# Linear attention: lengths and angles in groups among the projections, lookup and statistics among the pairs, an own output buffer; setup loads in another order

## The chip, the cores and the metric

The kernel runs on 1 core of one Trainium2 chip. The metric is the device time of one execution, in microseconds (us), lower is better.

## The reference, cut to what matters

2048 tokens of 512 features go through six residual layers. `_layernorm` and `ffn`, `attn` are as below; the change touches the second layer and what surrounds it.

```python
x = x + 0.5 * L0_ffn(layernorm(x))      # a lookup: each token picks one of 64 tiles, 8 features get a spline value
x = x + L0_attn(layernorm(x))           # linear attention
x = x + 0.5 * L0_ffn(layernorm(x))      # the same lookup
x = x + 0.5 * L1_ffn(layernorm(x))      # gate, up and down product with Hadamard-turned weights
x = x + L1_attn(layernorm(x))
x = x + 0.5 * L1_ffn(layernorm(x))

def L0_attn(x):                          # 4 sequences of 512, 16 heads of 32, 8 heads for k and v
    q, k, v = (x @ W.T + b for W, b in ...)
    q, k = rotate(q), rotate(k)          # q * cos + rotate_half(q) * sin
    def kernel(x):                       # length, projection, sine and cosine
        x = x / max(sqrt(sum(x * x)), 1e-6)
        p = x @ rand_matrix.T
        return concat(sin(p), cos(p)) / sqrt(32)
    kv = einsum('bhsf,bhsd->bsfd', kernel(k), v)      # for each token, over its heads
    out = einsum('bhsf,bsfd->bhsd', kernel(q), kv)
    return out @ Wo.T + bo
```

## The kernel before, in words

The program is written by hand for five queues: TensorE (pe), VectorE (V, dve), ScalarE (act), GpSimd (pool) and SyncE (sp), which issues all copies. Each queue runs in the order in which its code is written; named semaphores tie them. All tiles are cut by hand from one SBUF tensor, `arena`, and PSUM is one tensor `ps` of 8 banks of 512 floats, so rows of the trace read arena and ps, and it is the line that tells the operation.

The tokens are worked in 4 chunks of 512 (`NCH`). The stages, in order:

- **Setup** (`setup_*`): loads x and all weights, turns the weights by transposes (`first` for three groups of the attention weights, `turned` for the others, lines 776 and 917), mixes them with Hadamard matrices, and routes the first lookup. GpSimd mixes W_down, after ScalarE scaled it in `scale_down` (line 792). One set of statistics over all 16 token tiles (`setup_stats_vector`, `setup_scale_vector`, `setup_norm_vector`) feeds it. SyncE's order of loads is in `setup_sync`.
- **Linear attention** (`b_tensor`, `b_scalar`, `b_vector`, `b_pool`, `b_sync`), chunk by chunk. Per chunk: the products of the values (4 token tiles, line 1189, VectorE adds the bias at 1411); 6 blocks z of 128 rows for keys and queries, with 12 products each (1189), bias on ScalarE (1318), cosine product on GpSimd (1368), rotation product (1229), sine product and sum on VectorE (1421, 1422), square on GpSimd (1372) and sum of squares per head (1234), all six blocks into one bank. Then the lengths for all 24 heads at once: maximum (1430), root (1333) and `rsqrt_vector` (a reciprocal at 350 and three steps that refine it). Then for each block the angle product (1258), a product that spreads 1/length over the head's rows (1261), a copy (1330), multiply, round and subtract on VectorE (1439, 1445, 1447), the sine (1340), a cast (1343) and the low half (1451). `b_sync` sends values to DRAM and back, and issues 36 copies (1391) that put the features of the tokens side by side. Then 16 pairs of groups of tokens: scores (1277), mask on VectorE (1460), product with the values (1287); every four pairs ScalarE and VectorE split the result into a high and a low half (1354, 1485). It goes into `ht_hi` and `ht_lo`, the buffers that hold the chunk's normalized input. Last the output product (1189) and the residual (1475, 1478).
- Among this stands work for other chunks. `last` is the chunk before: its second statistics and routing (`token_stats_*`, `route_*`) stand among the projections. `next` is the chunk after: its first lookup (`apply_*`, `spline_vector`, lines 1035 to 1086) stands between the last low half and the pairs, and adding it to x (`add_vector`, 1002 to 1023) and the statistics (`norm_stats_vector`, `norm_scale_vector`) stand behind the pairs. Its transposes (`norm_tensor`, 1167, casts 1158 and 1127) stand behind the output product, in banks 0 and 1 in turn.
- Chunks 1 and 2 are one hardware loop (`Fori`), chunks 0 and 3 are written out. In the loop the semaphore values are registers (`gate`).
- Then the last routing, and four passes of the large products and the second attention, unchanged.

## Time and profile before

| | us |
|---|---|
| median of 3 runs (lowest, highest) | 2493.17 (2491.18, 2495.68) |
| the profiled execution, its own time | 2493.57 |
| its span in the trace | 2491.8 |
| busy in the span: TensorE, VectorE, ScalarE, GpSimd | 2077.4, 1250.5, 743.3, 200.6 |
| start of the first chunk's values, of the fourth's, of the stage behind the attention | 300.12, 745.57, 949.14 |

The profile is of one execution. An engine is busy while an instruction runs; register, semaphore and DMA-issuing instructions are not counted. The granted clock is that of TensorE as a share of 2.4 GHz. A row of the timeline merges neighbours of one line.

### The profile page before, as it was taken

Reading aid. Unit: us, or ns where it says so; the run is one execution under the profiler, and the core shown is the slowest. Engines: PE = TensorE matmul, PEld = TensorE weight load, DVE = VectorE, ACT = ScalarE, POOL = GpSimd, SP = SyncE. Lnnn points to the kernel's source line nnn. Section 1 sums busy time; section 2 is a strip of 40 time slices with the busy share of each in tenths; the row PEclk is TensorE's granted clock in tenths of the full one; section 3 lists DMA queues with packets and bytes.
Section 4 is the critical chain, followed back from the end, with each engine's and each line's share of the span. In section 5 each row is a group of like instructions: output and inputs, shape, how many; then the busy total and the mean of one; then the engine's idle time right before and its main releaser. Section 6 shows DMA issues by size and latency. Waiting matters only on the chain. (4 is left out here: it accounts for less than half of the span.)

```text
span 2491.8 us, 30544 instructions
## 1 busy us (share of the span) xinstructions
PE 2077.4 (83%) x12014; PEld 981.1 (39%) x12014; DVE 1250.5 (50%) x2301; ACT 743.3 (30%) x1146; POOL 200.6 (8%) x148
## 2 busy tenths in 40 slices
PE   4777477756658548999999999999999999999998
PEld 3444224223223224444444444444444444444443
DVE  4444456364464444645456625662567355633332
ACT  4443131223212312222323522352235223521211
POOL 3340010101002000000000101000100010000000
PEclk8777577767678668999999999999999999999999
DMA  6211420111001311222210211121112111222322
GB/s 255 68 51 17 167 37 22 7 39 17 23 16 17 106 69 62 97 96 85 77 43 29 77 56 35 34 77 51 42 35 77 51 43 34 71 74 100 104 99 87
DMA packets 90978, 158.70 MB, mean 64 GB/s; under 512 B 44182, under 2 KB 55772, under 8 KB 86108
## 3 DMA queue, kind: packets, MB, share of 16 engines
q1 hardware_dynamic: 90844, 156.86, 19.6%
q8 instruction: 91, 1.49, 0.2%
q14 instruction: 43, 0.35, 0.1%
HBM read 128.52 MB, written 18.87 MB: 59 GB/s over the span
## 5 line engine op out<-in xcount | busy, mean ns | idle before, releaser
L1189 PE MATMUL ps<-arena 128*128 128x512 f16 (+1 forms) x4512 | 1006.6, 379 | 30.5 <-DVE arena L1675 12.8
L1189 PEld LDWEIGHTS ps<-arena 128*128 128x128 f16 x4512 | 436.2, 99 | 533.4 <-issue 29.6
L1620 PE MATMUL ps<-arena 128*128 128x512 f16 x1536 | 347.8, 382 | 29.4 <-DVE arena L1666 16.2
L1620 PEld LDWEIGHTS ps<-arena 128*128 128x128 f16 x1536 | 147.2, 98 | 206.7 <-issue 28.1
L1642 ACT ACTIVATE arena<-ps,arena 128x512 f32<-128x512 f32 x128 | 87.7, 685 | 362.4 <-PE ps L1189 362.1
L1675 DVE SCALAR_TENSOR_TENSOR arena<-arena,ps 128x512 f32<-128x512 f32 x128 | 87.8, 686 | 210.2 <-ACT arena L1642 209.5
L2229 ACT ACTIVATE arena<-ps 128x1024 f32<-128x1024 f32 (+3 forms) x128 | 90.2, 705 | 251.9 <-PE ps L2138 251.9
L2334 DVE CAST arena<-arena 128x1024 f16<-128x1024 f32 (+3 forms) x128 | 66.6, 520 | 148.1 <-ACT arena L2229 146.1
L2300 DVE TENSOR_REDUCE arena<-ps 128x2 f32<-128x256 f32 (+3 forms) x128 | 99.5, 819 | 65.1 <-PE ps L2082 65.1
L1684 DVE SCALAR_TENSOR_TENSOR arena<-ps,arena 128x512 f32<-128x512 f32 x128 | 95.7, 748 | 39.8 <-PE ps L1189 39.8
L1703 DVE SCALAR_TENSOR_TENSOR arena<-ps,arena 128x512 f32<-128x512 f32 x64 | 44.0, 687 | 139.7 <-PE ps L1620 139.5
L2336 DVE TENSOR_TENSOR arena<-arena 128x1024 f16<-128x1024 f32 (+3 forms) x128 | 111.4, 870 | 4.4
L2280 POOL TENSOR_TENSOR arena<-arena 128x512 f16<-128x512 f32 x32 | 37.1, 1159 | 742.1 <-ACT arena L2207 742.1
L1666 DVE TENSOR_TENSOR arena<-arena 128x512 f16<-128x512 f32 x128 | 91.6, 715 | 4.0 <-ACT arena L1634 4.0
L1634 ACT ACTIVATE arena<-arena 128x512 f16<-128x512 f32 x128 | 79.7, 622 | 17.5 <-DVE arena L1684 17.5
L685 PE MATMUL ps<-arena 128*128 128x128 f32 x240 | 44.9, 347 | 46.5 <-DVE arena L917 27.5
L728 PE MATMUL ps<-arena 128*128 128x512 f16 x256 | 71.9, 450 | 5.7 <-DVE arena L917 5.7
L1277 PE MATMUL ps<-arena 96*128 96x256 f16 x128 | 29.2, 323 | 54.2 <-issue 32.0
L2136 PE MATMUL ps<-arena 32*128 32x512 f16 (+3 forms) x768 | 72.9, 293 | 0.0
L2204 ACT ACTIVATE arena<-ps 128x512 f32<-128x512 f32 x32 | 19.1, 597 | 166.7 <-PE ps L1189 166.7
L1460 DVE TENSOR_TENSOR arena<-ps,arena 128x256 f32<-128x256 f32 x128 | 47.3, 418 | 38.7 <-PE ps L1277 36.3
L2284 POOL TENSOR_TENSOR arena<-arena 128x512 f32<-128x512 f32 x16 | 18.6, 1163 | 580.2 <-DVE arena L2347 580.2
(266 smaller groups left out, 2442.5 us busy)
## 6 DMA issues: line engine op xcount, KB each, us to landing
arena<-wug_dram SPq DMA_DIRECT2D x128, 512.0 KB, 3.3
arena<-wd_hi_dram SPq DMA_DIRECT2D x16, 1024.0 KB, 5.0
arena<-wd_lo_dram SPq DMA_DIRECT2D x16, 1024.0 KB, 7.2
arena<-arena SPq DMA_DIRECT2D x144, 64.0 KB, 2.1
wug_dram<-arena SPq DMA_DIRECT2D x4, 2048.0 KB, 15.8
arena<-_attn_hidden_states_dram SPq DMA_DIRECT2D x4, 1024.0 KB, 10.4
arena<-in_L_ffn_W_down_dram SPq DMA_DIRECT2D x4, 1024.0 KB, 15.5
arena<-in_L_ffn_W_up_dram SPq DMA_DIRECT2D x8, 512.0 KB, 6.3
```

Source lines behind the costliest of these rows:

```text
L728: ins = pe.matmul(k.ps[:, bank, :], sign, part[:, jc, :], start=(n == 0), stop=(n == 7))
L1189: ins = pe.matmul(out, left[a](c), right[b](c), start=(at == 0), stop=(at == 3 * n - 1))
L1620: ins = pe.matmul(k.ps[:, bank, :], act[x][:, slot, cols], wd[y][:, f, :], start=(f == 0 and m == 0), stop=(f == 7 and m == 2))
L1634: e.activation(k.act_hi[:, g % ACT_SLOTS, :], k.prod[:, g % 2, :], ACT.Copy).then_inc(s["f_hi"], 1)
L1642: e.activation(k.th[:, g % 2, :], k.ps[:, GATE_BANK, :], ACT.Tanh, scale=k.wscale[:, FB + a:FB + a + 1])\
L1666: e.tensor_tensor(k.act_lo[:, g % ACT_SLOTS, :], k.prod[:, g % 2, :], k.act_hi[:, g % ACT_SLOTS, :], ALU.subtract)\
L1675: e.scalar_tensor_tensor(out=th, in0=th, scalar=1.0, in1=k.ps[:, GATE_BANK, :], op0=ALU.add, op1=ALU.mult)\
L1684: e.scalar_tensor_tensor(out=k.prod[:, g % 2, :], in0=k.ps[:, UP_HALF_BANK, :], scalar=k.wscale[:, a:a + 1], in1=th, op0=ALU.mult, op1=ALU ...
L2136: pe.matmul(k.ps[:, bank, queries], x[rows, 4 + b, keys], y[rows, b, queries], start=False, stop=False)
L2229: e.activation(k.p32[:, t % 2, :, queries], k.ps[:, 0:2, queries], ACT.Exp, scale=SCORE).then_inc(s["c_exp"], 1)
L2300: e.tensor_reduce(k.mx[:, u, 4 * b + 2 * j:4 * b + 2 * j + 2], k.ps[:, bank:bank + 2, 0:(u + 1) * P], AXX, ALU.max).then_inc(s["c_max"], 1)
L2336: e.tensor_tensor(k.p_lo[:, t % 2, :, queries], k.p32[:, t % 2, :, queries], k.p_hi[:, t % 2, :, queries], ALU.subtract).then_inc(s["c_p_l ...
```

## The change

**Setup.** SyncE loads Wk and Wv ahead of x, and each quarter of W_down (now with a semaphore of its own) behind a group of W_up. VectorE and ScalarE do the second group of attention weights ahead of the statistics, and the third ahead of the last step of them.

```diff
     load_nat(0, [(rows_of(d["L0_attn_Wq"])[:, 0:2], 2), (rows_of(d["L0_attn_Wq"])[:, 2:4], 2)])
+    load_nat(1, [(rows_of(d["L0_attn_Wk"]), 2), (rows_of(d["L0_attn_Wv"]), 2)])
     for c in range(NCH):
         sp.dma_start(k.x[:, c * TPC:(c + 1) * TPC, :],
                      d["L0_attn_hidden_states"][c].rearrange("(u p) n -> p u n", p=P)).then_inc(s[f"x_in{c}"], 16)
-    load_nat(1, [(rows_of(d["L0_attn_Wk"]), 2), (rows_of(d["L0_attn_Wv"]), 2)])
...
+        if g < 4:
+            sp.dma_start(k.wd_nat[:, g, :], d["L1_ffn_W_down"][g * P:(g + 1) * P, :]).then_inc(s[f"wd_in{g}"], 16)
...
     first(0)
+    first(1)
     setup_stats_vector(k, V)
     setup_scale_vector(k, V)
-    first(1)
+    first(2)
     setup_norm_vector(k, V)
-    first(2)
```

**Among the projections.** The six blocks are walked in 12 steps t: projection t, rotation t-1, sum of squares t-2, and from step 5 on angle and spreading product t-5. Lengths are taken for 2 blocks (8 heads) at a time, with the inverse root as exp(-0.5 ln) on ScalarE and three refining steps on VectorE. The angle product always goes to bank 5 and the spreading product to bank 1. The routing of the last chunk keeps its place among the steps, and the next chunk's lookup products come in steps 10 and 11.

```diff
+    for t in range(Z_STEPS):
...
+        z = t - 5
+        if 0 <= z < 6:
+            need(pe, s["b_y"], 6 * i + z)
+            pe.wait_ge(s["b_rope"], 6 * i + z + 1)
+            pe.matmul(k.ps[:, 5, :], k.rt, k.qr[:, z, :], start=True, stop=True).then_inc(s["b_proj"], 1)
+            need(pe, s["b_spread"], 6 * i + z)
+            pe.wait_ge(s["b_r"], 3 * i + z // 2 + 1)
+            at = P * (z % 2)
+            pe.matmul(k.ps[:, 1, :], k.spread[0:8, at:at + P], k.r2[0:8, z // 2 % 2, :], start=True, stop=True)\
+                .then_inc(s["b_p"], 1)
...
+    def inverse(g):
+        e.wait_ge(s["b_n2"], 3 * i + g + 1)
+        use_log(e)
+        e.activation(k.nr[0:8, 1, :], k.nr[0:8, 0, :], ACT.Ln).then_inc(s["b_ln"], 1)
+        e.wait_ge(s["b_ln"], 3 * i + g + 1)
+        e.activation(k.nr[0:8, 1, :], k.nr[0:8, 1, :], ACT.Exp, scale=-0.5).then_inc(s["b_n"], 1)
...
+        if t in (4, 6, 8):
+            inverse(t // 2 - 2)
+        if 0 <= t - 5 < 6:
+            spread(t - 5)
+        if t >= 6:
+            feature(t - 6)
+        if next is not None and t == 10:
+            apply_scalar(k, e, next, 1, LOOKUP_BANK)
+        if t == 10:
+            e.wait_ge(s["b_ks"], 192 * (i + 1))
+            keys(0)
+            keys(1)
```

`feature` is the sine and the cast, `keys` a regrouping of the keys. VectorE's order of the blocks is written out: rope(0) to rope(2), route_choice, lengths(0), rope(3), refine(0), rope(4), pick(0), pick(1), angle(0), lengths(1), rope(5), low(0), angle(1), pick(2), pick(3), refine(1), low(1), angle(2), lengths(2), low(2), angle(3), refine(2), low(3), angle(4), route_ends, low(4), angle(5), low(5), and then the first half of the lookup.

On ScalarE, in chunk 0 from the bias copies of the blocks on, before (1318 bias, 1333 root, 1330 copy of the spread lengths, 1340 sine, 1343 cast):

```order
L1318 ACTIVATE arena<-ps,arena 128x512 x6
L1333 ACTIVATE arena<-arena 24x512
L1330 ACTIVATE arena<-ps 128x512 x2
L1340 ACT_TABLE_LOAD
L1340 ACTIVATE arena<-arena 128x512
L1343 ACTIVATE arena<-arena 128x512
L1330 ACTIVATE arena<-ps 128x512
L1340 ACTIVATE arena<-arena 128x512
L1343 ACTIVATE arena<-arena 128x512
```

and now (1291 bias, 1811 `use_log`, 1279 Ln, 1281 Exp, 1267 copy, 1271 sine):

```order
L1291 ACTIVATE arena<-ps,arena 128x512 x5
L1811 ACT_TABLE_LOAD
L1279 ACTIVATE arena<-arena 8x512
L1281 ACTIVATE arena<-arena 8x512
L1291 ACTIVATE arena<-ps,arena 128x512
L1267 ACTIVATE arena<-ps 128x512
L1811 ACT_TABLE_LOAD
L1279 ACTIVATE arena<-arena 8x512
L1281 ACTIVATE arena<-arena 8x512
L1267 ACTIVATE arena<-ps 128x512
L1271 ACT_TABLE_LOAD
L1271 ACTIVATE arena<-arena 128x512
```

The root of all lengths has become three pairs of Ln and Exp, each with a table load ahead of it, and the sine's load comes twice, since the third pair stands between the sines.

**Among the pairs.** The rest of the next chunk's lookup, its addition to x and its statistics are cut in pieces, one after each mask.

```diff
+        if next is not None:
+            if y == 0:
+                spline_slope_vector(k, V, rows)
+            if y == 1:
+                spline_value_vector(k, V, rows)
+            if y == 2:
+                scale_start_vector(k, V, next)
+                scale_tiles_vector(k, V, next, range(2))
+            if y == 3:
+                scale_tiles_vector(k, V, next, range(2, TPC))
+            if 4 <= y < 8:
+                scatter_tile_vector(k, V, y - 4)
+            if 8 <= y < 12:
+                u = y - 8
+                xt = k.x[:, next * TPC + u, :]
+                V.link(e.tensor_tensor(xt, xt, k.scat[:, u, :], ALU.add))
+            if y >= 12:
+                norm_sums_vector(k, V, next, (y - 12,))
```

On VectorE in chunk 0, from the first mask on, before (1460 two masks a pair, 1485 low half):

```order
L1460 TENSOR_TENSOR arena<-ps,arena 128x256 x12
L1485 SCALAR_TENSOR_TENSOR arena<-ps,arena 128x64x8
L1460 TENSOR_TENSOR arena<-ps,arena 128x256 x8
L1485 SCALAR_TENSOR_TENSOR arena<-ps,arena 128x64x8
L1460 TENSOR_TENSOR arena<-ps,arena 128x256 x8
L1485 SCALAR_TENSOR_TENSOR arena<-ps,arena 128x64x8
L1460 TENSOR_TENSOR arena<-ps,arena 128x256 x4
L1485 SCALAR_TENSOR_TENSOR arena<-ps,arena 128x64x8
```

and now (1470 masks, 1075, 1066, 1068 slope and value, 1085 to 1087 their end, 1515 to 1517 start of the scaling):

```order
L1470 TENSOR_TENSOR arena<-ps,arena 128x256 x2
L1075 TENSOR_TENSOR arena<-arena 128x512
L1066 TENSOR_TENSOR arena<-arena,ps 128x256 x2
L1068 TENSOR_REDUCE arena<-arena 128x32
L1470 TENSOR_TENSOR arena<-ps,arena 128x256 x2
L1066 TENSOR_TENSOR arena<-arena,ps 128x256 x2
L1068 TENSOR_REDUCE arena<-arena 128x32
L1085 TENSOR_TENSOR arena<-arena 128x32
L1086 TENSOR_TENSOR arena<-arena 128x32
L1087 TENSOR_TENSOR arena<-arena 128x32
L1470 TENSOR_TENSOR arena<-ps,arena 128x256 x2
L1515 TENSOR_SCALAR arena<-arena 128x4
```

A mask used to follow a mask; now each has a piece of the next chunk behind it.

**Buffers and the rest.** The pairs' result goes to buffers of its own, `ot_hi` and `ot_lo`, which with `qs`, `ks`, `ksg`, `vr`, `sm` and `y2` now lie where the turned weights were; so the value copies wait for the stores of those weights, and the first ring loads of the next stage for the last pair. The next chunk's transposes take banks 0 to 3 without a wait between them, its statistics use Ln and Exp too, and VectorE subtracts their low halves behind the residual. Chunks 1 and 2 are written out as well.

```diff
+    b = k.wug_at
+    k.qs, b = v.at(b, [P, 16, CH], F16)
...
+    k.ot_hi, b = v.at(b, [P, KC, CH], F16)
...
-    sp.wait_ge(s["ug_out"], 16 * NCH)
+    sp.wait_ge(s["b_pv"], PAIRS * NCH)
...
+    if next is not None:
+        pe.wait_ge(s["ap_read"], next + 1)
     for u in range(TPC):
         cols = slice(u * P, (u + 1) * P)
-        pairs_product(pe, k.ps[:, OUT_BANK[u], :], [of(o, cols) for o in (k.ht_hi, k.ht_lo)],
+        pairs_product(pe, k.ps[:, OUT_BANK[u], :], [of(o, cols) for o in (k.ot_hi, k.ot_lo)],
                       [of(w, slice(1024, 1536)) for w in w0]).then_inc(s["b_out"], 1)
     if next is not None:
-        norm_tensor(k, pe, next, 1)
-    gate(pe, s["b_res"], nth(i, 1, TPC, TPC), s["gates"])
+        for c in range(KC):
+            turn_tensor(k, pe, next, c, TURN_BANK[c])
```

SyncE's loads from Wq on, before:

```order
L608 DMA arena<-in_L_attn_Wq_dram 128x2x512 x2
L622 DMA arena<-in_L_attn_hidden_states_dram 128x4x512 x4
L608 DMA arena<-in_L_attn_Wk_dram 128x2x512
L608 DMA arena<-in_L_attn_Wv_dram 128x2x512
L608 DMA arena<-in_L_attn_Wo_dram 128x2x512 x2
L627 DMA arena<-in_L_ffn_W_down_dram 128x2048 x4
L608 DMA arena<-in_L_ffn_W_up_dram 128x2x512 x8
```

and now:

```order
L613 DMA arena<-in_L_attn_Wq_dram 128x2x512 x2
L613 DMA arena<-in_L_attn_Wk_dram 128x2x512
L613 DMA arena<-in_L_attn_Wv_dram 128x2x512
L628 DMA arena<-in_L_attn_hidden_states_dram 128x4x512 x4
L613 DMA arena<-in_L_attn_Wo_dram 128x2x512 x2
L613 DMA arena<-in_L_ffn_W_up_dram 128x2x512 x2
L642 DMA arena<-in_L_ffn_W_down_dram 128x2048
L613 DMA arena<-in_L_ffn_W_up_dram 128x2x512 x2
L642 DMA arena<-in_L_ffn_W_down_dram 128x2048
L613 DMA arena<-in_L_ffn_W_up_dram 128x2x512 x2
```

Wk and Wv have moved ahead of x, and W_down's quarters behind two pieces of W_up each.

## Rows read from the trace of the kernel before

**Rows 1.** The page, part 2: busy tenths and granted clock in 40 slices of 62 us.

```profile
PE   4777477756658548999999999999999999999998
...
PEclk8777577767678668999999999999999999999999
```

**Rows 2.** Stages of the attention: from:to, length, busy us (and count) by engine, clock, DMA.

```profile
300.12:380.29 80.17, 56.76 (x181) 23.73 (x181) 37.13 (x67) 21.57 (x31) 12.58 (x12) 0.76 0.24 43
380.29:397.72 17.43, 16.14 (x288) 8.21 (x288) 13.22 (x35) 1.80 (x3) 0.00 (x0) 0.83 0.01 2
397.72:421.65 23.93, 14.47 (x64) 7.72 (x65) 19.94 (x40) 7.41 (x11) 0.00 (x0) 0.83 0.00 1
421.65:533.25 111.60, 71.09 (x257) 31.84 (x257) 49.67 (x105) 30.69 (x46) 12.64 (x12) 0.70 0.17 31
533.25:552.94 19.69, 16.39 (x288) 8.45 (x288) 13.78 (x35) 1.79 (x3) 0.00 (x0) 0.84 0.01 2
552.94:585.55 32.61, 14.41 (x65) 7.75 (x66) 20.04 (x40) 7.41 (x11) 0.00 (x0) 0.77 0.01 1
...
716.68:745.57 28.89, 14.41 (x66) 7.72 (x65) 20.03 (x40) 7.40 (x11) 0.00 (x0) 0.81 0.00 0
745.57:848.36 102.79, 65.87 (x244) 28.76 (x245) 42.60 (x83) 30.20 (x45) 12.62 (x12) 0.72 0.19 34
```

**Rows 3.** Timeline, chunk 0, one block's products: start, us, engine, line, operation.

```profile
317.93 2.77 PE L1189 MATMUL ps<-arena 128*128 128x512 f16 x12
...
320.54 1.02 PE L1229 MATMUL ps<-arena 128*128 128x512 f32 x2
...
321.49 1.04 PE L1234 MATMUL ps<-arena 128*24 128x512 f32 x2
```

**Rows 4.** Timeline, chunk 0, lengths and angles.

```profile
339.12 0.63 ACT L1333 ACTIVATE arena<-arena 24x512 f32<-24x512 f32 x1 [8.63 <-DVE arena L1430]
...
339.78 3.34 DVE L350 RECIPROCAL arena<-arena 24x512 f32<-24x512 f32 x1 [0.69 <-ACT arena L1333]
...
349.06 1.28 ACT L1340 ACT_TABLE_LOAD   x1
...
350.36 0.72 ACT L1340 ACTIVATE arena<-arena 128x512 f32<-128x512 f32 x1
...
353.35 2.07 PE L1261 MATMUL ps<-arena 24*128 24x512 f32 x2 [0.39 <-DVE arena L1439]
...
355.80 2.07 PE L1261 MATMUL ps<-arena 24*128 24x512 f32 x2 [0.38 <-DVE arena L1439]
```

**Rows 5.** Timeline, chunk 0, SyncE's copies of the features.

```profile
355.23 23.49 SPq L1391 DMA_DIRECT2D arena<-arena  x36
```

**Rows 6.** Timeline of TensorE, chunk 1: values and first two projections.

```profile
421.65 13.24 PE L1189 MATMUL ps<-arena 128*128 128x256 f16 x72 [1.95 <-DVE arena L1127]
```

**Rows 7.** Stage view: slope and value of the lookup; scaling to statistics, VectorE.

```profile
372.71:376.96 4.25, 0.00 (x0) 0.00 (x0) 4.01 (x8) 0.00 (x0) 0.00 (x0) 0.50 0.40 100
398.99:408.91 9.92, 9.74 (x46) 4.38 (x47) 9.70 (x17) 0.70 (x1) 0.00 (x0) 1.00 0.00 0
```

**Rows 8.** Timeline: output product and row scaling of chunk 0, output product of chunk 3.

```profile
399.17 10.53 PE L1189 MATMUL ps<-arena 128*128 128x512 f16 x48 [1.47 <-DVE arena L1485]
...
411.00 2.93 ACT L1148 ACTIVATE arena<-arena 128x512 f32<-128x512 f32 x4 [1.24 <-DVE arena L1118]
...
867.06 12.22 PE L1189 MATMUL ps<-arena 128*128 128x512 f16 x48 [1.44 <-DVE arena L1485]
```

**Rows 9.** Timeline of the setup: waits for weights, first split of W_up.

```profile
26.07 3.68 PE L685 MATMUL ps<-arena 128*128 128x128 f32 x16 [10.62 <-DMA arena<-in_L_attn_Wv_dram]
...
38.74 2.00 ACT L792 ACTIVATE arena<-arena 128x2048 f32<-128x2048 f32 x1 [3.12 <-DMA arena<-in_L_ffn_W_down_dram]
...
41.52 1.94 PE L685 MATMUL ps<-arena 128*128 128x128 f32 x8 [6.53 <-DMA arena<-in_L_ffn_W_up_dram]
...
43.27 0.69 DVE L917 SCALAR_TENSOR_TENSOR arena<-ps,arena 128x512 f16<-128x512 f32 x1 [6.12 <-ACT arena L776]
```

576 lines of the change are left out of this document (294 added, 282 removed).

## The prediction

> **What bounds the kernel now.** I read the page first, from its 40 slices [rows 1]: from slice 16 on, thus after about 940 us, TensorE is nine tenths busy or more and its granted clock is at nine tenths or more. The change leaves that part alone, so all that it can move lies before it. There TensorE is between four and eight tenths busy, and the clock with it. I then cut the linear attention into stages with the stage view [rows 2]. A chunk has three parts: from its first product of the values to the first pair score (A), the 16 pairs (B), and from the last pair to the next chunk's first product (C). In chunk 0 they take 80.2, 17.4 and 23.9 us. Chunk 1, which also routes the chunk before and runs inside a loop, takes 111.6, 19.7 and 32.6; chunk 2 repeats it but for a C of 28.9; chunk 3, written out and without a next chunk, has an A of 102.8. The reader is to see that no engine is busy through A: of 80.2 us in chunk 0 TensorE has 57 and VectorE 37. A is a chain that passes from engine to engine, and what counts is its length.
>
> That chain has three links. The projections run at TensorE's pace: 12 products in 2.77 us, a rotation 1.02 and a sum of squares 1.04, 4.53 us a block [rows 3]. Then come the lengths once for all six blocks, with a root of 0.63 and a reciprocal of 3.34 us, and then the angles, two blocks in flight, with 2.45 us from one spreading product at 353.35 to the next at 355.80, each of 2.07 us, TensorE's slow clock (half of 2.4 GHz) [rows 4]. Last come 36 copies on SP's queue, 23.49 us from the moment that two blocks are done; the pairs start 1.6 us after the last is issued [rows 5]. The lookup for the next chunk stands behind the angles on VectorE, and it costs nothing now: those copies take longer.
>
> **Part A after the change.** I walk through chunk 0 from the end of the values (7.3 us after its start, the rest of A being 72.9). TensorE's queue gives, with pitches of 2.6, 1.0 and 1.0 us [rows 3], 19.8 us to the end of step 4, 24.3 to the sum of squares in step 5, 26.3 with the first angle product and the first spreading product; with a copy on ScalarE and a multiply on VectorE the first angle is multiplied at 27.9. (A step over 512 columns is put at 0.6 to 0.65 us on ScalarE, after the root's 0.63 in [rows 4], and at 0.7 on VectorE, after the split's 0.69 in [rows 9].)
>
> From there the six angles run in a ring: bank 5 holds one angle product, so the next one waits for this multiply; the spreading product goes through bank 1; ScalarE copies block z+1 before it takes the sine of block z, and VectorE makes the low half of z before it multiplies z+1. One plain turn is two f32 products at the slow clock 4.1, copy 0.6, sine 0.72 and cast 0.65, low half 0.7, multiply 0.7, some 0.3 of handing over: 7.8 us, where before a block took 2.45 [rows 4]. Four of the five turns carry the lengths too. Turns 1 and 3 hold: rest of the angle 1.3, maximum 0.7, table load 1.28, Ln and Exp 1.3, copy 0.65, a second table load for the sine 1.28, sine and cast 1.4, low half and multiply 1.4, thus 9.3; turns 2 and 4 hold: rest 1.3, three refining steps 2.1, one slow product 2.05, copy, sine, cast, low half and multiply 3.5, thus 9.0. Sum of the five: 9.3+9.0+9.3+9.0+7.8 = 44.4, and 1.1 of handing over. To the last low half 3.4 more; 12 copies on SP are then still to be issued, 12 x 0.65 = 7.8, and 1.6 to land. 27.9+45.5+3.4+9.4 = 86.2 against 72.9: **13.3 us longer** in chunk 0.
>
> In chunks 1 and 2 the same walk starts later. The statistics of the last chunk and the routing stand among the projections before and after; written out, they lose the loop's extra steps, some 3 us. The first multiply comes 40 us after the values, turn 2 has two picks more (1.3), turn 3 the slice products between two others (it becomes 12.2), and the lookup's transpose sits ahead of the last sine: 102.2, with 6.7 us for the values, 108.9 against 111.6, 2.7 less each. In chunk 3, written out before too, it is 108.1 against 102.8, 5.3 more. The values' 6.7 is from [rows 6]: 72 products took 13.24 us where 48 of half the width and 24 of full width would take 10.5 at 2.77 per twelve, and I give half of that back, since TensorE comes from the output product more directly. A sums to 13.3-2.7-2.7+5.3 = **+13.2**.
>
> The trace shows the table load as 1.28 us and the sine starting 0.02 us behind it [rows 4]. The trace has no drain where the load follows a copy, so I take 1.28. The Trainium skill (ScalarE: Activation LUTs, What ACT_TABLE_LOAD costs) gives about 1.28 us for the load and 1.38 more for a drain at every switch; by the Trainium skill each of the four loads in the turns would be 2.66, an estimate of 5.5 us more a chunk. The same page advises to do all functions of one set before switching, which speaks against this change.
>
> **Part B.** Slope, value, scale, scatter, add and the four statistics go between the pairs of chunks 0 to 2. In the trace they are 4.25 and 9.92 us of VectorE, nearly without a gap [rows 7]; the add in four pieces costs 0.6 more: 14.8. In B VectorE is already busy for 13.2 of 17.4 us [rows 2], so little fits in: 13.2 of work, 14.8, and about 2.6 for handing over and the first score give 30.6. Against 17.4, 19.7 and 19.6 that is **+35.1**.
>
> **Part C.** What has gone to B was in C, but under the output product: 10.53 us of TensorE [rows 8]. C after: 1.5 to the first output product, 10.5 for the product, then the transposes into four banks, bounded by ScalarE's casts and VectorE's four subtractions, 4.3: 16.3. The statistics' tail, six short steps and four row scalings of together 2.93 [rows 8], some 5 us, lies under the product. Before, the transposes waited for the statistics and went two banks at a time. TensorE now comes out of pairs that keep it waiting, so I take 12.2 instead of 10.5, what the last chunk's product took [rows 8]: 18.0. Against 23.9, 32.6 and 28.9: **-31.4**. The own output buffer lets the transposes go as soon as the product is through; its worth is in this.
>
> **Setup.** Wk and Wv arrive before x, so the second group of weights is turned while TensorE used to wait 10.62 us [rows 9]. But VectorE has the low halves of that group (2.5 us) before its 16 statistics, x lands 1 MB later, and ScalarE's first scaling of W_down waits for the end of the same chain: I get 37.4 instead of 38.7. The first split of W_up on VectorE, at 43.27 before, then comes some 3 us sooner, since W_up no longer stands behind 4 MB. **-3.2**, with 0 and -6 as bounds: SP's reordered loads could gain nothing, or W_up's whole wait of 6.53 us. The first norm's transposes in four banks: **-0.6**. SP's value copies now also wait for the stores of the weights; those began 50 us before and I cost this at nothing. The ring loads of the next stage wait for the last pair, some 80 us before they are used: nothing.
>
> Sum: 13.2+35.1-31.4-3.2-0.6 = **+13.1** on the profiled execution's 2493.57 us, which is 0.4 above the median of the runs. 2493.2+13.1 gives 2506.
>
> **Rivals.** (1) Faster: TensorE keeps its fast clock through the ring. In [rows 3] a product of this size takes 1.0 us, so turns 2, 4 and 5 get 1, 1 and 2 us shorter, the output product 1.7, the values 1.5, chunk 1 to 3 gain 5 us in A and chunk 0 gains 4: 24 us less, 2482. It decides for faster once more than half of that comes. For it: more products are spread through A than before. Against: the angle loop before, with products nearly back to back, already ran at 2.07. (2) Cover in B: the new steps fall into waits that VectorE has anyway. With 4.2 idle us in each B, at most 12 in all, thus 2494, no change; with a larger gain in setup a little less. (3) Dearer: every handing over in the ring costs twice my figure, and each table switch a drain as well, 6 us a chunk: 2506 + 24 = 2530. For it: each turn passes TensorE, ScalarE and VectorE twice. Against: the handing over in [rows 4] is short. (4) The next chunk's lookup isn't ready when the pairs start, since its products stand behind the last spreading product; 10 us of copies cover its 7 us, so it costs nothing unless SP gets faster.
>
> **How the numbers follow.** My case 0.6; rival 1 and its neighbours 0.25; rival 2 0.1; rival 3 0.05. About 0.2%, 5 us, can be told from no change. Slower 0.65, same 0.1, faster 0.25. The range reaches from rival 1's 2482 to 2522, my case with 4 us more on each chunk's ring.
>
> **What would show it.** In the new profile: B of chunks 0 to 2 at 30 us with VectorE nearly full; C at 16 to 18; A of chunk 0 near 93 with five turns of 8 to 9 us and two table loads in two of them; the first split of W_up near 40. I am wrong if the turns take 6 us or if B stays near 20.

## The result, and the profile after

The changed kernel takes 2503.01 us (median of 6 runs, 2502.41 to 2505.37) against 2493.97 (6 runs, 2491.18 to 2495.68) of the kernel before: ratio 1.004, 95% interval 1.003 to 1.0051, 9 us slower. Of the forecast's +13.1 most came, but the profile shows that it didn't come all from where I put it. The profiled execution after has 2505.37 us and a span of 2503.6, 11.8 more than the span of before.

First the page of after, its 40 slices, to be held against [rows 1]. The slow stretch is again slices 1 to 16, and its clock is lower in the middle.

```profile
PE   4877466858768547999999999999999999999998
...
PEclk7777666758567668999999999999999999999999
```

Then the stage view of after, cut at the same events as [rows 2]: from:to, length, busy us (and count) of TensorE, its weight loads, VectorE, ScalarE, GpSimd, then clock, DMA share, GB/s.

```profile
293.79:384.87 91.08, 60.63 (x181) 22.73 (x182) 35.79 (x67) 29.81 (x40) 13.08 (x12) 0.70 0.22 38
384.87:414.04 29.17, 18.20 (x288) 8.64 (x288) 27.34 (x64) 1.79 (x3) 0.00 (x0) 0.62 0.01 1
414.04:431.65 17.61, 13.65 (x66) 6.73 (x65) 9.99 (x23) 7.29 (x12) 0.00 (x0) 0.88 0.00 1
431.65:542.36 110.71, 77.99 (x257) 35.00 (x258) 46.26 (x105) 40.34 (x56) 12.61 (x12) 0.67 0.17 31
542.36:571.51 29.15, 19.31 (x288) 8.90 (x288) 27.34 (x64) 1.79 (x3) 0.00 (x0) 0.50 0.01 1
571.51:590.58 19.07, 15.10 (x65) 7.11 (x65) 9.99 (x23) 7.29 (x12) 0.00 (x0) 0.81 0.00 1
590.58:699.53 108.95, 76.19 (x256) 34.10 (x257) 46.27 (x105) 40.34 (x56) 12.62 (x12) 0.68 0.17 32
...
747.66:856.39 108.73, 71.37 (x245) 31.09 (x246) 43.72 (x90) 39.85 (x55) 12.61 (x12) 0.68 0.17 32
```

The reader is to see VectorE 27.3 of 29.2 us busy in the pairs (second row) where it had 13.2 of 17.4, and the clock of a chunk's first part down from 0.76 to 0.70. Set against the forecast:

| part | before | after | difference | forecast |
|---|---|---|---|---|
| A, chunks 0, 1, 2, 3 | 80.2, 111.6, 111.6, 102.8 | 91.1, 110.7, 109.0, 108.7 | +13.3 | +13.2 |
| B, chunks 0, 1, 2 | 17.4, 19.7, 19.6 | 29.2, 29.2, 29.1 | +30.8 | +35.1 |
| C, chunks 0, 1, 2 | 23.9, 32.6, 28.9 | 17.6, 19.1, 19.0 | -29.7 | -31.4 |
| first value product | 300.1 | 293.8 | -6.3 | -3.8 |
| from chunk 3's first score to the end | 1643.4 | 1647.2 | +3.8 | 0 |

One profile places such a stage only to some 3 us. The kernel of the run e12_delay below has the same code as after up to the end of the attention; its four A's sum to 416.7 where those of after sum to 419.5, and its last pair ends at 870.8 for 873.7.

The last row is the surprise. I split it at the first gate activation of the next stage on ScalarE (a tanh, line 1642 of before and 1694 of after; VectorE makes the gate's sigmoid of it, and I call it the first sigmoid), which begins at 953.7 in the trace of before and at 958.9 in that of after: up to there the changed kernel is 5.2 us late. The other 6.6 us of the 11.8 arise behind it, in code that the change leaves alone. Two rows of the stage view of before, the stage that ends at 2050.3 being the second attention with its woven neighbours:

```profile
953.70:1237.80 284.10, 274.13 (x1283) 126.55 (x1281) 146.35 (x283) 74.24 (x113) 2.32 (x2) 0.99 0.26 89
1237.80:2050.30 812.50, 771.70 (x5054) 347.46 (x5051) 449.36 (x716) 276.59 (x433) 63.12 (x54) 0.99 0.15 50
```

And the same stretches, between the same instructions, of after:

```profile
958.90:1243.20 284.30, 274.23 (x1285) 126.60 (x1283) 146.91 (x292) 74.21 (x113) 2.31 (x2) 0.99 0.26 90
1243.20:2062.00 818.80, 777.96 (x5053) 349.62 (x5050) 449.38 (x716) 276.48 (x433) 63.10 (x54) 0.98 0.15 49
```

VectorE, ScalarE and GpSimd do the same work; TensorE is busy 6.3 us longer at a lower clock, 0.98 for 0.99. The experiments take this up again.

The ring of the angles in chunk 0, TensorE's timeline of after (start, us, engine, line, operation, idle before and its releaser). L1173 is the sum of squares, L1179 the angle product, L1183 the spreading product:

```profile
328.64 1.02 PE L1173 MATMUL ps<-arena 128*8 128x512 f32 x2 [2.27 <-DVE arena L1383]
329.60 2.08 PE L1179 MATMUL ps<-arena 128*128 128x512 f32 x2
331.61 2.07 PE L1183 MATMUL ps<-arena 8*128 8x512 f32 x2
...
338.39 2.08 PE L1179 MATMUL ps<-arena 128*128 128x512 f32 x2 [2.91 <-DVE arena L1399]
341.75 2.04 PE L1183 MATMUL ps<-arena 8*128 8x512 f32 x2 [1.28 <-DVE arena L1392]
347.08 2.08 PE L1179 MATMUL ps<-arena 128*128 128x512 f32 x2 [3.28 <-DVE arena L1399]
349.08 2.07 PE L1183 MATMUL ps<-arena 8*128 8x512 f32 x2
356.02 2.08 PE L1179 MATMUL ps<-arena 128*128 128x512 f32 x2 [4.87 <-DVE arena L1399]
```

From 338.39 on, every angle product waits for the multiply of the block before (L1399): the products start 8.8, 8.7 and 8.9 us apart. Before, spreading products followed each other by 2.45 us [rows 4]. The turn ahead of these is the longest. Its sum of squares (first row) stands in TensorE's queue ahead of the angle product and waits for the maximum of the second group (L1383), so between the multiplies of blocks 0 and 1 there are 11.6 us:

```profile
326.06 0.69 DVE L1399 SCALAR_TENSOR_TENSOR arena<-ps,arena 128x512 f32<-128x512 f32 x1 [1.59 <-ACT arena L1267]
...
337.65 0.68 DVE L1399 SCALAR_TENSOR_TENSOR arena<-ps,arena 128x512 f32<-128x512 f32 x1
```

A later turn (from block 2 to block 3) on ScalarE and VectorE:

```profile
348.88 1.28 ACT L1811 ACT_TABLE_LOAD   x1 [3.19 <-DVE arena L1383]
350.18 0.63 ACT L1279 ACTIVATE arena<-arena 8x512 f32<-8x512 f32 x1
350.84 0.63 ACT L1281 ACTIVATE arena<-arena 8x512 f32<-8x512 f32 x1
351.37 0.57 ACT L1267 ACTIVATE arena<-ps 128x512 f32<-128x512 f32 x1
351.96 1.28 ACT L1271 ACT_TABLE_LOAD   x1
353.26 0.72 ACT L1271 ACTIVATE arena<-arena 128x512 f32<-128x512 f32 x1
354.01 0.63 ACT L1274 ACTIVATE arena<-arena 128x512 f16<-128x512 f32 x1
354.67 0.69 DVE L1413 SCALAR_TENSOR_TENSOR arena<-arena 128x512 f16<-128x512 f32 x1 [5.81 <-ACT arena L1274]
355.28 0.68 DVE L1399 SCALAR_TENSOR_TENSOR arena<-ps,arena 128x512 f32<-128x512 f32 x1
```

The first table load with Ln and Exp ends at 351.47 (350.84 + 0.63), only 0.3 us behind the spreading product (349.08 + 2.07 = 351.15), which the copy waits for in any case. So in this turn that load lies beside TensorE; only the sine's load stands alone on the chain.

### The profile page after: what moved, and what is told of

The parts are those of the page before. It is cut to its first block and busy times, and to the rows that moved or that the text cites. A ratio compares the mean times of both kernels' runs of the same rounds, so it can differ in the third digit from the quotient of the medians.

```text
span 2503.6 us, 29624 instructions
## 1 busy us (share of the span) xinstructions
PE 2108.1 (84%) x12014; PEld 986.9 (39%) x12014; DVE 1254.7 (50%) x2358; ACT 780.7 (31%) x1190; POOL 201.0 (8%) x148
## 3 DMA queue, kind: packets, MB, share of 16 engines
q1 hardware_dynamic: 90844, 156.86, 19.6%
## 5 line engine op out<-in xcount | busy, mean ns | idle before, releaser
L1101 PE MATMUL ps<-arena 128*128 128x512 f16 (+1 forms) x4512 | 1011.1, 380 | 31.1 <-DVE arena L1727 12.9
L1101 PEld LDWEIGHTS ps<-arena 128*128 128x128 f16 x4512 | 435.1, 98 | 537.4 <-issue 32.6
L1672 PEld LDWEIGHTS ps<-arena 128*128 128x128 f16 x1536 | 147.6, 98 | 207.9 <-issue 30.2
L1686 ACT ACTIVATE arena<-arena 128x512 f16<-128x512 f32 x128 | 79.7, 622 | 17.5 <-DVE arena L1736 17.5
L1179 PE MATMUL ps<-arena 128*128 128x512 f32 x48 | 45.9, 1057 | 44.8 <-DVE arena L1399 44.8
L690 PE MATMUL ps<-arena 128*128 128x128 f32 x240 | 43.2, 337 | 42.9 <-DVE arena L922 30.2
L1413 DVE SCALAR_TENSOR_TENSOR arena<-arena 128x512 f16<-128x512 f32 x24 | 16.6, 692 | 114.1 <-ACT arena L1274 114.1
L1221 PE MATMUL ps<-arena 96*128 96x256 f16 x128 | 34.8, 375 | 45.1 <-issue 45.1
L2256 ACT ACTIVATE arena<-ps 128x512 f32<-128x512 f32 x32 | 19.1, 597 | 166.7 <-PE ps L1101 166.7
## 6 DMA issues: line engine op xcount, KB each, us to landing
arena<-_attn_hidden_states_dram SPq DMA_DIRECT2D x4, 1024.0 KB, 11.8
```

The source lines that it names most:

```text
L1101: ins = pe.matmul(out, left[a](c), right[b](c), start=(at == 0), stop=(at == 3 * n - 1))
L1672: ins = pe.matmul(k.ps[:, bank, :], act[x][:, slot, cols], wd[y][:, f, :], start=(f == 0 and m == 0), stop=(f == 7 and m == 2))
L1686: e.activation(k.act_hi[:, g % ACT_SLOTS, :], k.prod[:, g % 2, :], ACT.Copy).then_inc(s["f_hi"], 1)
```

## The experiments

All kernels ran beside the kernel before on their own chip; ratios are to it. "First sigmoid" is when the unchanged stages begin in the profiled execution, "behind" the time from there to the last sigmoid, the same instructions in all; both are of one execution. The kernel before had medians of 2493.9 to 2496.1 beside the others.

| kernel | median us | ratio, 95% interval | first sigmoid | behind |
|---|---|---|---|---|
| before | 2493.97 | | 953.7 | 1506.9 |
| after | 2503.01 | 1.004 (1.003 to 1.0051) | 958.9 | 1513.5 |
| e5_setup_alone | 2490.58 | 0.9981 (0.9972 to 0.999) | 947.0 | 1510.4 |
| e4_pairs_clear | 2485.38 | 0.9957 (0.9944 to 0.997) | 939.8 | 1513.4 |
| e3_no_tables | 2498.96 | 1.0008 (0.9999 to 1.0017) | 953.5 | 1513.5 |
| e2_banks_order | 2463.90 | 0.9871 (0.9857 to 0.9886) | 928.7 | 1504.0 |
| e1_banks_only | 2491.72 | 0.9991 (0.9982 to 1.0) | 947.7 | 1510.2 |
| e8_filled | 2489.60 | 0.9988 (0.9978 to 0.9997) | 953.4 | 1503.7 |
| e6_shared_out | 2504.74 | 1.004 (1.0026 to 1.0054) | 958.4 | 1513.4 |
| e7_both | 2450.28 | 0.9811 (0.9794 to 0.9829) | 907.0 | 1511.0 |
| e10_lengths_first | 2430.45 | 0.9757 (0.974 to 0.9773) | 887.4 | 1510.1 |
| e14_first_filled | 2432.66 | 0.9742 (0.973 to 0.9755) | 890.3 | 1513.4 |
| e12_delay | 2498.43 | 1.0019 (1.001 to 1.0028) | 958.8 | 1503.8 |
| e13_before_delay | 2497.91 | 1.0008 (0.9999 to 1.0018) | 954.0 | 1513.3 |

**The setup alone**, on the kernel before:

```diff
+    load_nat(1, [(rows_of(d["L0_attn_Wk"]), 2), (rows_of(d["L0_attn_Wv"]), 2)])
...
-    load_nat(1, [(rows_of(d["L0_attn_Wk"]), 2), (rows_of(d["L0_attn_Wv"]), 2)])
...
-    for o in range(4):
-        sp.dma_start(k.wd_nat[:, o, :], d["L1_ffn_W_down"][o * P:(o + 1) * P, :]).then_inc(s["wd_in"], 16)
...
+        if g < 4:
+            sp.dma_start(k.wd_nat[:, g, :], d["L1_ffn_W_down"][g * P:(g + 1) * P, :]).then_inc(s[f"wd_in{g}"], 16)
```

> The kernel before with the setup part of the change alone (order of the loads, Wk and Wv turned before the statistics, W_down's pieces between the blocks of W_up). Theory A, from the two traces: the attention's first value product starts 6.33 us sooner after the change, 1.3 of them in the transposes into four banks, which this kernel does not have; so 5.0 us less, 2489. Theory B, as predicted: 3.2 less, 2490.8. Theory C, the attention only starts sooner and gives it back in its first copies: no difference, 2494.

Measured: 0.9981, 4.9 us less by the medians. Theory A stands in size. The forecast's 3.2 was on the low side: the first split of W_up on VectorE went from 43.27 [rows 9] to 39.07 (38.47 in the kernel after), 4.2 sooner, and the first value product from 300.12 to 293.80, 6.3 sooner. That is where the kernel after has it (293.79), though this kernel lacks the transposes into four banks, so their share of 1.3 us, or 0.6 in the forecast, is not seen. In the twelve profiles with this setup the first value product comes at 293.0 to 295.5, in the two without it at 300.1 and 299.6. This part of the change is a gain.

**The pairs left clear**, on the kernel after: slope and value go ahead of the pairs, the rest behind them.

```diff
         spline_place_vector(k, V, next, 1, rows)
+        spline_slope_vector(k, V, rows)
+        spline_value_vector(k, V, rows)
     for y in range(PAIRS):
...
-            if y == 2:
-                scale_start_vector(k, V, next)
-                scale_tiles_vector(k, V, next, range(2))
...
     b_low(k, e, i, 3)
     if next is not None:
+        scale_start_vector(k, V, next)
+        scale_tiles_vector(k, V, next, range(TPC))
...
```

> The kernel after with the next chunk's slope and value ahead of the pairs (under the copies) and its scale, scatter, addition and statistics behind them (under the output product), as before the change; everything else stays. Theory A: the steps among the pairs are a plain loss, since VectorE is full there. The 16 pairs of chunks 0 to 2 fall from 29.2 us to about 17.5; behind them 9.9 us of VectorE, its tail and four row scalings of some 5 us now end 1.5 to 4 us after the output product of 12 to 13 us, so the stretch behind grows by 3 to 5 us. Net 7 to 9 us a chunk in three chunks: 2478 to 2482. Theory B: what leaves the pairs comes back in full behind them (the trade is even): 2500 to 2505. Theory C: the pairs get no shorter, since something else than VectorE paces them: slower than the kernel after, 2515.

Measured: 0.9957, some 20 us less than the kernel after; the first sigmoid comes 19.1 sooner. Theory A, a little under its 21 to 27 us. Chunk 0 of this kernel, first its pairs in the stage view, then TensorE's timeline behind them (L1101 the output product, L1581 the transposes):

```profile
386.10:403.60 17.50, 16.17 (x288) 8.26 (x288) 13.24 (x35) 1.80 (x3) 0.00 (x0) 0.82 0.01 2
```

```profile
405.05 10.53 PE L1101 MATMUL ps<-arena 128*128 128x512 f16 x48 [1.47 <-DVE arena L1532]
420.86 3.68 PE L1581 MATMUL ps<-arena 128*128 128x128 f32 x16 [5.27 <-ACT arena L1796]
426.55 0.82 PE L1101 MATMUL ps<-arena 128*128 128x256 f16 x3 [2.01 <-DVE arena L1596]
```

The pairs take 17.5 instead of 29.2, the stretch behind 22.9 instead of 17.6 (403.6 to 426.55): 6.3 less in chunk 0, and 8.0 and 7.9 in chunks 1 and 2 by the same sum. The transposes do wait for the statistics now, by 5.27 us, but pairs longer by 11.7 us were dearer. In all runs that keep the crowded pairs these take 29.1 to 29.2 us, at granted clocks from 0.50 to 0.62: TensorE's clock does not pace them, VectorE does. The output product has its 10.53 us again, as in [rows 8]. In the kernel after, behind the crowded pairs of chunks 0 and 1, TensorE's timeline has

```profile
415.54 11.90 PE L1101 MATMUL ps<-arena 128*128 128x512 f16 x48 [1.50 <-DVE arena L1540]
...
573.02 13.35 PE L1101 MATMUL ps<-arena 128*128 128x512 f16 x48 [1.51 <-DVE arena L1540]
```

where the pairs just ahead ran at a clock of 0.62 and 0.50.

**No tables in the ring.** The inverse lengths are two scaled copies on ScalarE instead of Ln and Exp, so this kernel leaves out the true inverse lengths.

```diff
-        use_log(e)
-        e.activation(k.nr[0:8, 1, :], k.nr[0:8, 0, :], ACT.Ln).then_inc(s["b_ln"], 1)
+        e.activation(k.nr[0:8, 1, :], k.nr[0:8, 0, :], ACT.Copy, scale=1e-4).then_inc(s["b_ln"], 1)
```

> The kernel after, where the inverse length on ScalarE (Ln, Exp) is two scaled copies of the same size, so that no table is loaded between the sines of a chunk; the lengths are then not the reference's. Theory A, by my terms: two loads of 1.28 us in each of two turns of the ring, all of it on the chain: 10.2 us less over four chunks for the sine's loads and as much for the other, 20.5 in sum, 2482.5. Theory B, read from the trace after: the first load of a turn, with Ln and Exp, ends only 0.2 us after the spreading product that the next copy waits for, so it costs nearly nothing, and the sine's load costs its 1.28: 1.5 us in eight turns, 12 us less, 2491. Theory C: the turns are paced by TensorE's products and the multiply alone: less than 3 us, 2500 to 2503. By the Trainium skill (ScalarE: Activation LUTs) a switch costs a drain besides, 2.66 us; by that the four loads in the turns of a chunk would be worth 43 us, an estimate of that page.

Measured: 1.0008, and a first sigmoid 5.4 us sooner than in after. My terms (20.5 us) fall, and B was twice too high as well. The reason stands in its timeline: of the two turns in chunk 0 that hold lengths, the first keeps its load for the sine, which is the chunk's first; only the second loses one and takes 7.36 us (356.13 from 348.77) instead of 8.94 (356.02 from 347.08), 1.6 less. Four chunks would give 6.3, and the first sigmoid says 5.4, with the scatter of 3 us between profiles. By the Trainium skill (ScalarE: Activation LUTs, What ACT_TABLE_LOAD costs) there is a drain with each switch; the trace disagrees: the load starts with the copy's end (351.37 + 0.57, then 351.96), the sine 0.02 us after the load, and the turn gets shorter by little more than the load's 1.28.

**Banks and order.** Three banks for the angle products, two for the spreading products; on VectorE the angle of block z+1 ahead of the low half of z. Since bank 4 is also the rotation's, the third spreading product waits for all six rotations, and the lookup's products wait for the last angle.

```diff
+ANGLE_BANK = (5, 2, 3, 5, 2, 3)
+SPREAD_BANK = (1, 1, 4, 1, 4, 1)
...
-            need(pe, s["b_y"], 6 * i + z)
+            need(pe, s["b_y"], 6 * i + max(z - 2, 0))
...
-    low(0)
-    angle(1)
+    angle(1)
+    low(0)
```

> The kernel after with a looser ring: angle products through three banks (5, 2, 3), spreading products through two (1, 4), and on VectorE the angle of block z+1 ahead of the low half of block z. Theory A: the ring of single buffers made the turns of 8.8 us. What then paces a turn is TensorE's two products at the slow clock, 4.15 us, or in the turns with lengths ScalarE with 5.8 (two loads, Ln, Exp, copy, sine, cast): about 5.5 on average instead of 8.6, 15 us less in chunk 0, and about half of that in the chunks with routing: 35 to 45 us less, 2458 to 2468. Theory B: the lengths (maximum, table loads, Ln, Exp, refinement) pace the turns however many buffers there are: under 10 us less, 2493 to 2500. Theory C: the last 12 copies on SP and the landing take up what is gained: no difference.

Measured: 0.9871, 41 us less than the kernel after; 30.2 of them up to the first sigmoid, and 9.5 behind it. By the sum that is theory A's size; by the trace the attention gives 30 of it. So the ring was a loss of single buffers and order, as I had worked it out, and not of the lengths alone (B) nor hidden by the copies (C). The order alone, with single banks, was not run.

**Banks only**: the first part of that edit, with VectorE's order unchanged.

```diff
+ANGLE_BANK = (5, 2, 3, 5, 2, 3)
+SPREAD_BANK = (1, 1, 4, 1, 4, 1)
...
-            need(pe, s["b_y"], 6 * i + z)
+            need(pe, s["b_y"], 6 * i + max(z - 2, 0))
```

> The kernel after with the banks of the looser ring alone, VectorE's order unchanged (low half of block z ahead of the angle of block z+1). Theory A: the single buffers were the whole loss; what is left of a turn is multiply, two roundings, sine, cast and low half, 4.1 us with the handing over, not longer than TensorE's two products: within 4 us of the run with banks and order, 2464 to 2468. Theory B: VectorE's order is half of it: 2478 to 2486.

Measured: 0.9991, first sigmoid 11.2 sooner than after, 19 later than with the order. Theory B, and stronger than I had put it. In chunk 0 TensorE (L1181 the angle product, L1187 the spreading product) no longer waits for a bank:

```profile
344.92 2.07 PE L1187 MATMUL ps<-arena 8*128 8x512 f32 x2
346.92 2.08 PE L1181 MATMUL ps<-arena 128*128 128x512 f32 x2
358.57 2.04 PE L1187 MATMUL ps<-arena 8*128 8x512 f32 x2 [9.58 <-DVE arena L1397]
```

It waits 9.58 us for a refined length (L1397), which on VectorE stands behind a low half, which waits for ScalarE, which waits for the lengths' own maximum. A buffer more moves the wait to the next thing that is queued in order; my expectation (within 4 us of banks and order together) had counted one turn's steps and not what is queued behind a waiting one.

**TensorE's waits filled** in the kernel after, with eight products that nobody reads, in four turns of each chunk:

```diff
+        if 6 <= t < 10:
+            for m in range(8):
+                pe.matmul(k.ps[:, 2, :], k.w0_hi[:, m % 4, 0:P], k.ht_hi[:, m % 4, :], start=(m == 0), stop=(m == 7))
```

> The kernel after with eight more products of 128x512 f16 into a free bank behind the spreading product in four of the six turns of each chunk; nobody reads them. TensorE waited 2.9 to 4.9 us there for VectorE. Theory A (the slow clock is what makes the ring long, and work would bring the fast one back): the turn's two products fall from 4.1 to 2.1 us, the eight lie in the wait, 2 us less a turn: up to 30 us less than the kernel after, 2475 to 2490. Theory B: the clock stays at its lower level in the ring; eight products of about 0.43 us take 3.4 and hardly fit: 0 to 1 us more a turn, 2504 to 2520.

Measured: 0.9988, some 15 us less than the kernel after, within theory A's range. Its timeline in chunk 0 shows the fast clock coming back for two turns, and going again once a wait of 4.54 us stays unfilled:

```profile
343.32 1.09 PE L1183 MATMUL ps<-arena 8*128 8x512 f32 x2 [2.23 <-DVE arena L1395]
344.34 2.93 PE L1187 MATMUL ps<-arena 128*128 128x512 f16 x8
...
349.12 1.12 PE L1183 MATMUL ps<-arena 8*128 8x512 f32 x2
350.18 1.92 PE L1187 MATMUL ps<-arena 128*128 128x512 f16 x8
356.64 2.08 PE L1179 MATMUL ps<-arena 128*128 128x512 f32 x2 [4.54 <-DVE arena L1402]
```

But only 5.5 of the 15 us lie ahead of the first sigmoid, not far above the scatter of one profile. The other 9.8 are again in the unchanged stages, 1503.7 for 1513.5. More work on TensorE can so be worth time, but less than the sum of this run says.

**Output in the shared buffer**, on the kernel after:

```diff
-    k.ot_hi, b = v.at(b, [P, KC, CH], F16)
-    k.ot_lo, b = v.at(b, [P, KC, CH], F16)
+    k.ot_hi, k.ot_lo = k.ht_hi, k.ht_lo
```

> The kernel after with the attention's output in the buffer of the normalized tokens again, as before, instead of in a buffer of its own. Theory A, against my prediction's sentence that the buffer lets the transposes go: TensorE transposes behind its output product in any case, and the casts follow the transposes, so the buffer is worth nothing: as the kernel after, 2503 to 2507 here. Theory B, as predicted: the buffer carries part of the gain behind the pairs: 4 to 6 us a chunk, 2515 to 2523.

Measured: 1.004 (1.0026 to 1.0054), as the kernel after. Theory A: the own buffer is worth nothing.

**Ring and pairs together**, the two edits above in one kernel.

> The looser ring and the pairs left clear together. The ring alone gave 41 us against the kernel after and the pairs alone 20. Theory A: the two lie in different stages of a chunk and add up: 61 less than the kernel after, 2444 to 2448 on this chip; the stages behind the attention may add or take 6 us, as they did between the runs so far. Theory B: the stages share something, since a looser ring sends the copies on SP earlier and the next chunk's slope and value then no longer lie under them: 2450 to 2456.

Measured: 0.9811, 2450.28. The first sigmoid is 51.9 sooner than after's; the two alone gave 30.2 and 19.1. Up to there they add up (theory A). The median is in theory B's range, and its five runs lie at two levels, 2440.87 and 2443.28, and 2450.28 to 2450.97; the profiled execution is of the upper one, with 1511.0 in the stages behind where the ring alone had 1504.0. This kernel beats both the kernel before and after.

**Lengths first**, on top of that: all three groups are inverted and refined ahead of the first spreading product, with `k.r2` three deep and the spreading products at `z = t - 7`.

```diff
-        if t in (4, 6, 8):
+        if t in (4, 6):
             inverse(t // 2 - 2)
+        if t == 7:
+            inverse(2)
...
+    refine(1)
+    lengths(2)
     pick(2)
     pick(3)
-    refine(1)
+    refine(2)
+    angle(0)
```

> The kernel with the looser ring and the clear pairs, where moreover all three groups of lengths are inverted and refined before the first spreading product, so that no table load and no refinement stands between the angles; the angle products run two steps ahead of the spreading products, a third buffer holds the refined lengths. Theory A: the lengths inside the ring are what still makes two of its turns long (7.7 and 8.6 us against 3.9 to 4.1 for the others, in chunk 0): the first angle comes 6 to 8 us later, but the five turns then take 4.1 each instead of 29.6 together, so 3 to 6 us less a chunk, 2434 to 2442. Theory B: what is gained in the ring is lost ahead of it: 2450, as the kernel without this. Theory C: the first copies on SP start later and their queue of 23.5 us paces the chunk: 2450 to 2460.

Measured: 0.9757, 2430.45, the fastest of the study: 19.6 less up to the first sigmoid than without. Theory A, at more than its size. The turns are 5.56 us now, two slow products and a wait for the multiply:

```profile
337.38 2.08 PE L1181 MATMUL ps<-arena 128*128 128x512 f32 x2 [4.08 <-DVE arena L1407]
339.38 2.07 PE L1189 MATMUL ps<-arena 8*128 8x512 f32 x2
342.94 2.08 PE L1181 MATMUL ps<-arena 128*128 128x512 f32 x2 [1.49 <-DVE arena L1407]
```

Part A of chunks 1 to 3 gets 5.7 to 7.0 us shorter and that of chunk 0 nothing (the pairs start at 375.4 for 374.7): the first copy leaves later there, at 350.32 for 345.82, and the 36 copies need 23.5 us. The copies now set the end of A in every chunk.

**The same with the waits filled**:

```diff
+        if 7 <= t < 11:
+            if t == 7:
+                pe.wait_ge(s["b_n2"], 3 * i + 3)
+            n = 12 if t == 7 else 5
+            for m in range(n):
+                pe.matmul(k.ps[:, 0, :], k.w0_hi[:, m % 4, 0:P], k.ht_hi[:, m % 4, :], start=(m == 0), stop=(m == n - 1))
```

> The kernel with lengths first, with unread products of 128x512 f16 into bank 0 where TensorE waits in the ring: twelve behind the first spreading product of a chunk (it waited 4.1 us there), five behind each of the next three (1.5 us). Theory A: the fast clock comes back as it did in the filled kernel; a turn of 5.6 us, of which 4.1 are two products at the slow clock, falls to about 4.5, paced by the chain through ScalarE and VectorE: 3 to 6 us less a chunk, 2408 to 2420. Theory B: the fillers run at the slow clock, five take 2.1 us for a wait of 1.5, and the ring gets 2 to 3 us longer a chunk: 2434 to 2442.

Measured: 2432.66, ratio 0.9742 (0.973 to 0.9755) against 0.9757 (0.974 to 0.9773): the intervals overlap. Neither theory, but the clock did return, and with it turns of 3.66 us:

```profile
339.69 1.13 PE L1181 MATMUL ps<-arena 128*128 128x512 f32 x2
340.75 1.12 PE L1189 MATMUL ps<-arena 8*128 8x512 f32 x2
341.80 1.26 PE L1196 MATMUL ps<-arena 128*128 128x512 f16 x5
343.35 1.13 PE L1181 MATMUL ps<-arena 128*128 128x512 f32 x2 [0.29 <-DVE arena L1413]
...
373.94 1.01 PE L1234 MATMUL ps<-arena 96*128 96x256 f16 x4 [13.13 <-issue]
```

The ring ends sooner and the first score hardly moves (373.94 for 375.45): TensorE sits idle for 13.13 us ahead of it. In SP's own timeline of this kernel the copies run without a gap:

```profile
348.84 23.49 SPq L1376 DMA_DIRECT2D arena<-arena  x36
```

348.84 and 23.49 and 1.6 to land are 373.9. In chunks 1 to 3 the copies take 22.96 or 22.97 us from 486.75, 623.45 and 760.03, and the scores start at 511.33, 648.09 and 784.65, again 1.6 behind their end. The granted clock of A rose from 0.73 to 0.76 without the fillers to 0.78 to 0.82, and the four A's sum to 369.8 for 370.5. Once the ring is quick, SP's copies set the end of part A, and TensorE's clock is worth next to nothing there. The later first sigmoid, 890.3 for 887.4, arises behind the last chunk's first score, which comes 0.2 us sooner; no run says why.

**A pure delay**, in the kernel after and in the kernel before: the four statistics at the start of the stage behind the attention are done twice.

```diff
     norm_sums_vector(k, V, 0, range(TPC))
+    norm_sums_vector(k, V, 0, range(TPC))
     norm_spread_vector(k, V)
```

> The kernel after with the four statistics at the start of the stage behind the attention done twice, 2.5 us more of VectorE where everything waits for VectorE; the results are the same. The question is what the unchanged stages behind do when they begin at another time: in the profiles so far they took 1503.7 to 1513.5 us from their first sigmoid on, in steps of about 3.3. Theory A: these steps belong to the position of the program against the chip's clock control, so that a shift alone moves them: the stages behind then differ from 1513.5 by 3 us or more, and the sum of the run is not 2.5 more. Theory B: they do not depend on the start: 2.5 us more, 2507, and 1513.5 again.

> The same doubled statistics (2.5 us of VectorE at the start of the stage behind the attention) in the kernel before. Its stages behind took 1506.9 us from their first sigmoid in the profile. Theory A: the time of the unchanged stages depends on when they start, so they move by one or more of the 3.3 us steps between 1503.7 and 1513.5, in either direction, and the run by something other than 2.5. Theory B: the kernel before is 2.5 slower, 2496.5, with 1506.9 again.

Measured: the kernel after with 2.5 us of work more is not slower but some 5 us faster, 1.0019 (1.001 to 1.0028) against 1.004 (1.003 to 1.0051), with its slowest run (2500.72) below the fastest of after (2502.41; the kernel before had 2493.9 and 2494.0 beside them), and its stages behind took 1503.8 instead of 1513.5. So theory B falls for the kernel after. For the kernel before the runs decide nothing: the median moved by 1.9, from which 2.5 can't be told, and the twelve runs lie in two groups, 2492.67 to 2495.87 and 2499.95 to 2502.82. The profiled execution is of the upper group, with 1513.3 instead of 1506.9.

Theory A isn't shown either. The stages behind began at 958.8 with the delay and at 958.9 without, since the attention ahead of it happened to take less, and yet they took 1503.8 and 1513.5. In the four profiles in which they began between 953.4 and 954.0 they took 1503.7, 1513.5, 1506.9 and 1513.3. Their place in the program's time does not select the step, and the two groups of runs suggest that one kernel can take different ones.

What the steps consist of the traces do show: TensorE's clock where the stages change over. Before, and then after, in stretches of 25 us:

```profile
1437.80:1462.80 25.00, 20.29 (x94) 9.53 (x94) 5.63 (x9) 3.15 (x6) 0.00 (x0) 0.93 0.07 22
1637.80:1662.80 25.00, 22.76 (x184) 10.15 (x184) 19.06 (x40) 12.27 (x19) 2.09 (x2) 1.00 0.13 43
```

```profile
1443.20:1468.20 25.00, 20.30 (x87) 9.46 (x88) 5.56 (x9) 3.07 (x6) 0.00 (x0) 0.86 0.06 22
1643.20:1668.20 25.00, 22.76 (x158) 9.61 (x158) 19.36 (x38) 11.71 (x18) 2.09 (x2) 0.93 0.15 50
```

The granted clock is 0.93 and 1.00 there, then 0.86 and 0.93. A mean lower by 0.07 is 14% of 25 us, 3.5 us, more at the slow level, so some 1.75 us of work lost; between 1390 and 1970 us there are four such differences, 7 us in sum against the 6.3 measured. Over the whole stretch from first to last sigmoid the clock record of the traces holds some 10 us at the slow level in the three profiles with 1503.7 to 1504.0, 17 in that with 1506.9, 24 in those with 1510.1 to 1510.4, 27 with 1511.0 and 31 in the six with 1513.3 to 1513.5; 9.7 us more of time go with 20.5 more at half the clock. By the Trainium skill (TensorE: Matmul & The Clock Gate, What's actually happening) the gate's watch runs freely and does not start with the kernel; these profiles fit that, since the same code, begun at the same time of the program, was slow for 10 us or for 31, but no run isolates it.

## Why the prediction was right, and where not

**The bound** was read rightly: all that moved by design lay ahead of 950 us. (The slices at nine tenths begin with the 17th, at 997 us, not with the 16th.)

**Part A, +13.2, came as +13.3**: +10.9, -0.9, -2.6 and +5.9 by chunk for +13.3, -2.7, -2.7 and +5.3. With the A's of e12_delay, which is the same code, it would be +10.5, so the agreement to 0.1 us is luck. The ring was the mechanism; the runs with banks and order show it by 30 us. My five turns of chunk 0 were 9.3, 9.0, 9.3, 9.0 and 7.8, with the handing over 45.5; between the multiplies there were 11.6, 8.7, 8.9, 8.9 and 7.35, again 45.5 in sum. Chunk 0 came 2.4 under its 13.3 for another reason, 2.0 of it in its first 72 products: they took 10.61 us at a granted clock of 1.00 where before they had 12.59 at 0.84, and I had left them as they were.

The step that failed inside is the chain of turns 1 and 3, those with table loads: I had it on ScalarE and VectorE alone, with both loads on it. In the trace it runs through TensorE. In turn 1 a sum of squares waits for the maximum, and two products at the slow clock follow, 11.6 us for my 9.3. In turn 3 the load with Ln and Exp lies beside two slow products of 4.07 us (to within 0.3), and the two ways are nearly as long, 8.9 for 9.3. The run without the tables gave some 6 us, not 20.

**Part B, +35.1, came as +30.8.** VectorE was full, as forecast, with 27.3 us instead of 28.0; the 2.6 us that I gave for handing over were 1.8. That this is a loss is shown by the kernel with clear pairs.

**Part C, -31.4, came as -29.7.** The output product was the mis-sized term: 12.2 us in the forecast, 11.90, 13.35 and 13.29 in the trace, behind pairs that ran at a clock of 0.62, 0.50 and 0.55; with clear pairs at 0.82 it took 10.53. The sentence that gave the own buffer a worth was wrong: the shared one did as well.

**Setup, -3.8 with the first transposes, came as -6.3 in the profile**; alone it measured -4.9 by the medians and -6.3 at the first value product, for the -3.2. The outer bound of -6 was nearer.

So the changed stretch up to the first sigmoid was 5.2 us slower, not 13.1: B came 4.3 lower, setup 2.5, the stage behind the last chunk's first score 2.8 (which may be scatter: this stage, less the delay, took 103.4 us in e13_before_delay, 105.3 in before and 102.5 in after), and C gave 1.7 less back. The median's 9 us comes nearer to the forecast because the unchanged stages added to it, 6.6 us in the profiled executions, a term that the forecast put at nothing. Without it the change would, by the profile, have cost some 5 us, at the edge of what the forecast called no change. The direction of each part was understood; that the sum came out near was in part luck.

**The rivals.** (1) The fast clock did not come by itself: 0.50 all through the ring. Its mechanism is real, since filled waits brought the clock back, but it was worth some 5.5 us here up to the first sigmoid and not 24. (2) Cover in B: no, 20 us were lost by moving the steps there. (3) Dearer hand-overs: no. (4) The lookup was never late; the idle time ahead of the first score is SP's.

## What to carry to other kernels

When work is moved between stages, ask of each stage which engine is full in it: VectorE had no room among the pairs, and 14.1 us of work put there made them 11.7 us longer. When a chain runs over several engines, give each hand-over two buffers and check also the order within each engine's queue; more banks alone gave 11 us, banks and order 30. Ask also what stands ahead of a product in TensorE's queue: one sum of squares that waited for a maximum made the first turn the longest. After each gain look for the next bound before the next edit: once the ring was quick, SP's 36 copies set the end and a faster TensorE clock was worth next to nothing.
